# Layer 2's scan: one instruction of 1024 columns for both halves of a unit, the seam set by ScalarE, and 11 instead of 12 of 32 states weighed by GpSimd

## What is computed

```python
# layer 2, after group norm, projection, 3x3 convolution and silu
# xs: 4 directions (rows, columns, both reversed), L = 4096 positions, d = 256
dt = softplus(dts + dt_proj_b)
def step(h, inp):                      # once per position l
    dA = exp(dt_l[..., None] * A)      # decay
    h = h * dA + (dt_l * u_l)[..., None] * B_l[:, :, None, :]   # drive
    y = einsum("bkdn,bkn->bkd", h, C_l)                         # weighing, sum over states
```

## Time and profile before

| what | value |
|---|---|
| median of 3 runs | 40399.08 us |
| the profiled execution | 40396.46 us |
| its span, first to last instruction | 40394.6 us |
| busy VectorE (DVE) | 33936.9 us, 84% |
| busy GpSimd (POOL) | 30996.0 us, 77% |
| busy TensorE matmul (PE) | 29251.1 us, 72% |
| busy ScalarE (ACT) | 19958.1 us, 49% |
| line 1568, scans of layer 2 | 16384 instructions |
| mean granted TensorE clock | 0.875 of full speed |

### The profile page before, as it was taken

The page is one execution under the profiler, slowest core; times in us unless marked ns, Lnnn a source line. Parts: engine busy times, 40 slices in busy tenths (PEclk is TensorE's granted clock), DMA queues, the critical chain, the costliest instruction groups (busy, mean ns, idle before and its releaser), DMA issues. The chain is left out here.

```text
span 40394.6 us, 270531 instructions
## 1 busy us (share of the span) xinstructions
PE 29251.1 (72%) x61476; PEld 11541.5 (29%) x61476; DVE 33936.9 (84%) x33869; ACT 19958.1 (49%) x37509; POOL 30996.0 (77%) x14776
## 2 busy tenths in 40 slices
PE   6777777777777777777777777777777777777777
PEld 3232232322323223232232322323223232232322
DVE  7969879698796987969879698796987969879698
ACT  4545545455454554545545455454554545545455
POOL 6949869498694986949869498694986949769497
PEclk8888888888888888888888888888888888888888
DMA  3424324243242432424324243242432424324243
GB/s 104 151 83 152 135 100 151 85 151 134 100 152 84 152 134 101 152 84 152 134 102 151 83 152 134 101 152 84 151 133 103 151 84 151 133 102 152 84 152 132
DMA packets 1387317, 5029.10 MB, mean 124 GB/s; under 512 B 164272, under 2 KB 165816, under 8 KB 1381440
## 3 DMA queue, kind: packets, MB, share of 16 engines
q1 hardware_dynamic: 1385536, 5010.20, 35.5%
HBM read 4938.25 MB, written 71.30 MB: 124 GB/s over the span
## 5 line engine op out<-in xcount | busy, mean ns | idle before, releaser
L662 PE MATMUL PS<-WORK,CST 128*128 128x512 f32 x36096 | 19792.8, 693 | 8395.9 <-POOL WORK L556 7606.2
L545 POOL TENSOR_TENSOR WORK<-WORK,XN 128x1024 f32<-128x1024 f32 x8192 | 19253.1, 2383 | 1.3
L662 PEld LDWEIGHTS PS<-WORK,CST 128*128 128x128 f32 x36096 | 7532.0, 220 | 20965.6 <-POOL WORK L556 10427.4
L1026 ACT ACTIVATE PS<-WORK,AN 128x512 f32<-128x512 f32 x17408 | 11307.0, 679 | 1984.9 <-DVE WORK L1576 1092.8
L1568 DVE TENSOR_TENSOR_SCAN PS<-PS,HST,WORK 128x512 f32<-128x512 f32 x8960 | 10975.2, 1272 | 45.4 <-ACT PS L1026 32.1
L1568 DVE TENSOR_TENSOR_SCAN WORK<-PS,HST,WORK 128x512 f32<-128x512 f32 x5376 | 6582.9, 1267 | 0.0
L556 POOL TENSOR_TENSOR WORK<-WORK,CWIDE 128x1024 f32<-128x1024 f32 x2048 | 4864.0, 2375 | 118.3 <-issue 65.2
L1026 ACT ACTIVATE HST<-PS 128x2 f32<-128x2 f32 x5152 | 858.6, 167 | 6586.2 <-DVE WORK L1576 6152.6
L632 POOL MEMSET XN<- 128x66 f32 x32 | 4.9, 154 | 5101.7 <-DVE SM L1414 5003.0
L1576 DVE TENSOR_TENSOR WORK<-PS,WORK 128x1024 f32<-128x1024 f32 x3072 | 3763.0, 1225 | 105.2
L1026 ACT ACTIVATE WORK<-PS 40x512 f32<-40x512 f32 (+2 forms) x1600 | 935.5, 598 | 3547.7 <-PE PS L662 2867.3
(11 more groups left out here) (158 smaller groups left out, 25260.5 us busy)
## 6 DMA issues: line engine op xcount, KB each, us to landing
XN<-xbc_rows SPq DMA_DIRECT2D x4096, 512.0 KB, 3.6
WORK<-xbc_rows SPq DMA_DIRECT2D x2816, 512.0 KB, 4.3
CWIDE<-xbc_rows SPq DMA_DIRECT2D x2304, 512.0 KB, 4.2
BIG<-in_spec_dram SPq DMA_DIRECT2D x32, 2048.0 KB, 12.3
X<-in_x_dram SPq DMA_DIRECT2D x68, 512.0 KB, 4.8
xbc_rows<-WORK SPq DMA_DIRECT2D x512, 64.0 KB, 3.1
out_dram<-X SPq DMA_DIRECT2D x64, 512.0 KB, 5.1
xbc_rows<-WORK SPq DMA_DIRECT2D x128, 32.0 KB, 1.6
```

The source lines that it names most:

```text
L545: nc.gpsimd.tensor_tensor(S.both(S.Q[u % 6]), S.both(S.DU[u // SN % 2]), S.wide(S.BW, u).unsqueeze(1).to_broadcast([P, 2, NT]), MUL).then_ ...
L662: return nc.tensor.matmul(o, w, r, start=start, stop=stop)
L1026: return nc.scalar.activation(o, i, f, **k)
```

## The change

- `states(u)` issues one scan of 1024 columns over both banks of the unit and all of its Q. The two halves lie one behind the other, so the state would run on from the first half into the second.
- ScalarE therefore sets the seam: in the first column of the half that comes second (column 512, or 511 for the reversed directions) `seam(u)` puts drive + decay x carried state into the drive's buffer (Identity with two pointer operands, only where c > 0), and 0 into the decay. It runs after decays(u+1) in the loop, ahead of split, softplus and carry. It waits for both decays, and with c > 0 for the unit's drive and for the carry of the chunk before; then for its own first operation.
- The scan waits for both decays and for the seam, where before the first half waited for its own decay alone.
- `POOL_STATES` is now taken over 32 units: six states in a group with even c, five (without n = 12) in one with odd c. SyncE's order is not touched.

```diff
--- before.py
+++ after.py
@@ -24,7 +24,7 @@
 RANK = 8
 GROUPS = 32
 POOL_STATES3 = (2, 5)
-POOL_STATES = (1, 4, 6, 9, 12, 14)
+POOL_STATES = (1, 4, 6, 9, 12, 14, 17, 20, 22, 25, 30)
 
 
 def shape_constants():
@@ -244,6 +244,8 @@
 
 
 
+
+
             units = KDIR * NCH * SN
             pool = POOL_STATES
 
@@ -273,6 +275,7 @@
                 s.du_ready = sample_sem("s2_du_ready")
                 s.decay = sample_sem("s2_decay")
                 s.drive = sample_sem("s2_drive")
+                s.seamed = sample_sem("s2_seamed")
                 s.scanned = sample_sem("s2_scanned")
                 s.carried = sample_sem("s2_carried")
                 s.weighed_dve = sample_sem("s2_weighed_dve")
@@ -286,7 +289,7 @@
 
             def on_pool(s, u):
 
-                return u % SN in s.pool
+                return u % (2 * SN) in s.pool
 
             def weighed_by_pool(s, u):
 
@@ -296,6 +299,15 @@
 
                 k, c, n = s.of(u)
                 return (k * (NCH - 1) + c) * SN + n + 1
+
+            def seams(s, u):
+
+                return sum(2 if s.of(v)[1] else 1 for v in range(u + 1))
+
+            def long(s, u):
+
+                lo = s.banks(u)[0]
+                return PS[:, lo:lo + 2, :].rearrange("p b l -> p (b l)")
 
             def wait_weighed(s, e, u):
 
@@ -1185,6 +1197,19 @@
                         act(bank(S.banks(u)[h]), S.DT[u // SN % 2][:, ch(h)], ACT.Exp,
                             scale=AN2[:, col:col + 1]).then_inc(S.decay, 1)
 
+                def seam(u):
+
+                    k, c, n = S.of(u)
+                    col, h = (NT, 1) if k < 2 else (NT - 1, 0)
+                    a, b = S.long(u)[:, col:col + 1], S.Q[u % 6][:, col:col + 1]
+                    e.wait_ge(S.decay, 2 * u + 2)
+                    if c:
+                        e.wait_ge(S.drive, u + 1)
+                        e.wait_ge(S.carried, S.carried_by(u - SN))
+                        act(b, a, ACT.Identity, scale=HST2[:, 2 * n + h:2 * n + h + 1], bias=b).then_inc(S.seamed, 1)
+                        e.wait_ge(S.seamed, S.seams(u) - 1)
+                    act(a, a, ACT.Copy, scale=0.0).then_inc(S.seamed, 1)
+
                 def carry(u):
 
                     k, c, n = S.of(u)
@@ -1203,10 +1228,12 @@
                     for part in range(3):
                         softplus(0, h, part)
                 decays(0)
+                seam(0)
                 for u in range(S.units):
                     g, n = u // SN, u % SN
                     if u + 1 < S.units:
                         decays(u + 1)
+                        seam(u + 1)
                     if g + 1 < KDIR * NCH:
                         if n == 2:
                             split(g + 1)
@@ -1556,17 +1583,15 @@
 
                     k, c, n = S.of(u)
                     e.wait_ge(S.drive, u + 1)
+                    e.wait_ge(S.decay, 2 * u + 2)
+                    e.wait_ge(S.seamed, S.seams(u))
                     if c:
                         e.wait_ge(S.carried, S.carried_by(u - SN))
-                    q = S.Q[u % 6]
-                    for h in range(2):
-                        e.wait_ge(S.decay, 2 * u + h + 1)
-                        a, b = bank(S.banks(u)[h]), q[:, ch(h)]
-                        o = b if S.on_pool(u) else a
-                        if k >= 2:
-                            a, b, o = a[:, ::-1], b[:, ::-1], o[:, ::-1]
-                        r = V.tensor_tensor_scan(o, a, b, HST2[:, 2 * n + h:2 * n + h + 1] if c else 0.0, MUL, ADD)
-                    r.then_inc(S.scanned, 1)
+                    a, b, first = S.long(u), S.Q[u % 6], 2 * n
+                    o = b if S.on_pool(u) else a
+                    if k >= 2:
+                        a, b, o, first = a[:, ::-1], b[:, ::-1], o[:, ::-1], first + 1
+                    V.tensor_tensor_scan(o, a, b, HST2[:, first:first + 1] if c else 0.0, MUL, ADD).then_inc(S.scanned, 1)
 
                 def weigh(u):
```

## The result

The changed kernel took 40779.74 us, the median of 4 runs (40775.77 to 40781.5), against 40402.26 of before (4 runs): ratio 1.0094, 95% interval 1.0077 to 1.0112. The profiled execution spans 40777.2 us, 382.6 more than before, 23.9 an image. The forecast was 40,530, 0.32% slower.

A forecast was written before the change was run, and what follows sets the result against it. Layer 2's scan was taken as bound by full GpSimd and a ring through carry(9). Middle chunks +10.1 us, c = 7 -2, c = 0 nothing: +8.1 an image, +130 in all, 40,530 us; likeliest 40,330 to 40,700, wide range 40,050 to 40,880.

The forecast's parts named there:

- The ring: Layer 2's scan, take_y to take_y through carry(9): almost no slack in directions 1 and 3, about 1 us in 0 and 2.
- The scan: VectorE's one scan of 1024 columns: 2.34 us against 2.46 for a pair, 0.13 saved a state with the semaphore.
- The seam: Identity then Copy on ScalarE between decays and scan: 0.58 us, bounds 0.40 to 0.80, holding ScalarE as long.
- the stalls before n = 7, 9 and 10: VectorE waiting for ScalarE, late from softplus and seams: 0.75, 0.1 and 1.05 us, together about 1.95 a group.
- The odd groups: Groups with odd c: ring 2.31 us shorter, VectorE's own work last, 55.55 us (+0.02) and 56.71 (+0.26).
- likeliest case: The forecast itself, ScalarE late through the seams: 40,330 to 40,700 us, chance 0.43.
- a seam of 0.72 us: Part of rival "More than reckoned" (chance 0.19): a longer seam adds 270 us, giving 40,800.
- a scan that saves nothing: Part of rival "More than reckoned" (chance 0.19): a 1024 scan without saving adds 470 us, giving 41,000.
- the groups of c = 7: Last chunk of a direction: no carry, stalls halve, directions 0 and 2 win 1 us each, -2 us an image.
- those of c = 0: First chunk of a direction: the seam is one Copy, GpSimd stays full, change 0.
- GpSimd alone: Rival: GpSimd sets the pace, seam short or hidden in ScalarE's waits; 590 us go, 39,810 us, chance 0.13.
- The table load: Rival: each Identity in a seam causes table loads, at least 10,800 us more, 51,000 us, chance 0.02.

The follow-up runs named there:

- The longer seam: Changed kernel with a second Copy in each seam, behind a wait for the first, no value changed: 41146.68 us, 1.0194 of the kernel before.
- the two runs with two scans at n = 5 to 10: Changed kernel, states n = 5 to 10 scanned in halves without seam; GpSimd keeps 11 of 32 states (40252.88 us, 0.9973) or 12 (40329.33 us, 0.999).
- both gaps filled: Changed kernel plus unused PE matmuls: three before the n=14 sum in odd groups, two before the take_y that follows: 40621.03 us, 1.0062 of before.
- without any seam: Kernel before with GpSimd weighing 11 of 32 states, two scans everywhere: 40469.75 us, 1.0027 of before.
- once the seams were hidden: Changed kernel with two scans and no seam at n = 5 to 10, 11 of 32 states on GpSimd: 40252.88 us, 0.9973 of before.
- with PE kept busy: Changed kernel, two scans and no seam at n = 5 to 10, 11 of 32 states on GpSimd, unused matmuls in both PE gaps: 40129.28 us, 0.994.

## Why the prediction was right, and where its size was off

- *What bounds.* The ring take_y, scans, carry(9), weighing of n=9, PE, take_y was there with the slacks read from the trace: even groups of 55.98 and 57.63 us in directions 2 and 1, against 55.86 and 57.53 forecast. Those of direction 0, taken as those of direction 2, came to 56.2 to 56.3.
- *GpSimd.* It lost its 2.31 us in odd groups, and the kernel gained nothing by it, as forecast, but in part for another reason (below).
- *The scan.* 2.351 us against 2.34; a state is 0.11 us shorter for it, not 0.13.
- *The seam.* ScalarE's 0.55 us against 0.58. The longer seam shows that five of them lie in the ring, the two runs with two scans at n = 5 to 10 that the other ten cost nothing. One term was mis-sized: from the end of Copy to the scan it is 0.19 us, not 0.02. With it the P states take 2.46 instead of 2.30 us, which puts a stall of 0.20 before n = 5 and n = 15, and the stalls before n = 7, 9 and 10 come out at 0.57, 0.26 and 0.98 (forecast 0.75, 0.1, 1.05). These are differences of starts; the rows show 0.09 less as idle, because neighbours overlap by that much. Together they make 2.21 us in an odd group, against the 1.95 forecast.
- *The odd groups* are the step that failed: "the ring is 2.31 shorter, so VectorE's own work is last: 55.55 and 56.71". They took up to 56.72 and 58.3. Part of it is VectorE's own work: with both gaps filled it is 56.1 to 56.4 and 57.28, 0.57 to 0.86 us more than forecast. In directions 1 and 3 those 0.57 come out of the two terms above: 0.26 more stalls, and 16 x 0.02 = 0.3 less saved by the scans. The rest is a term the sum did not have: PE at half clock in the sums of n = 14 and 15, +2.9 us on the ring. It made the ring last again, and so cost 0.8 to 1.0 us in the groups of c = 3 and 5 of directions 1 and 3 and 0.3 to 0.4 in direction 2, nothing in direction 0. I had taken PE's time behind the last weighing from the rows of even groups and had not asked when PE would stand idle once the weighing of n=12 had left.
- *The total.* Forecast +130 us, measured +377, almost three times as much. The likeliest case's own range, 40,330 to 40,700, did not hold it; the wide range did, and in part by luck: it reached up to 40,880 for a seam of 0.72 us or a scan that saves nothing, and neither came. The clock accounts for about 129 of the missing 247 (run with both gaps filled against the changed kernel), VectorE's odd groups at about 0.65 us x 12 x 16 = 125 for the rest; this last part is a sum from group times, no run takes it apart. The ends of a direction were off too, and the two nearly cancel: the groups of c = 7, forecast 2 us an image shorter, came out 0.9 longer (in directions 0 and 2 they take 56.3 and 56.6 us, and 54.9 with both gaps filled, so the half clock reached them too); those of c = 0, forecast unchanged, came out 1.1 shorter.
- *Rivals.* "GpSimd alone" was said to hold if the seam is short or hidden. It fell for this kernel, and without any seam it fell too (1.0027). A part of its gain showed once the seams were hidden: 0.9973, and 0.994 with PE kept busy, against the 0.985 that it would give. The table load did not occur.

## What to carry to other kernels

Work that is cheap on a half-idle engine is not cheap where another engine waits for it. A dependent pair of tiny ScalarE operations, 0.55 us long, cost 1.2 us a group in directions 1 and 3, and each 0.19 us added to it cost 0.95 more, because it sat five times in one chain of waits. Apply such an edit where the chain has slack and leave the old form elsewhere; here six of sixteen states made the difference between 1.009 and 0.997. And when work moves between engines, look at who is idle before the last step that the loop waits for, not only at who got freed.

## What the runs showed of the hardware

- TensorE's granted clock was 0.50 (1.2 GHz) in the first 3.3 us of the sums behind 3.96 us of idling, and in those behind 2.66 us (x4 in 3.75 us); in the sums behind 1.61 us it was 1.00, and with 2.7 us of matmuls put into the gap it was 1.00 too. The two sums that others wait for took 6.60 instead of 3.70 us by it.
- The length of the idling just before does not tell the clock by itself: the sums below, in the changed kernel, stand behind 1.54 us and ran at 0.50 for 3.41 us (PE's timeline and window).

```profile
3717.59 5.40 PE L674 MATMUL PS<-WORK,CST 128*128 128x512 f32 x8 [1.54 <-POOL WORK L568]
```

```profile
3718.61:3722.02 3.41, 3.41 (x6) 1.35 (x5) 2.93 (x2) 3.35 (x9) 3.41 (x2) 0.50 0.45 150
```

- One column through ScalarE with two pointer operands takes 0.351 us and blocks it for 0.38; without pointers 0.156.
- The scans that waited for a one-column ScalarE write started 0.19 to 0.20 us after its end.
- VectorE's scan of 1024 columns took 2.351 us, two of 512 took 2.44 to 2.46: the second start was worth 0.1 us.
